# Row sums of the attention from one tile instead of two, and projections one step later

## The reference

```python
xn = layernorm(x)
c  = layernorm_64((xn @ W_to_kv.T) @ W_compress.T) * gamma + beta
q, k, v = rope(c @ Wq.T), rope(c @ Wk.T), c @ Wv.T
o  = softmax(causal(q @ k.T / 8)) @ v
z  = o @ W_comp2lat.T
out = x + z @ W_to_kv + z @ W_out.T + b_out + ffn(xn)   # ffn: shared part + 2 of 16 experts
```

## Time and profile before

| what | value |
|---|---|
| median of 3 runs | 1843.62 us (1842.06 to 1844.86) |
| the profiled execution | 1834.49 us |
| its span, first to last instruction | 1832.7 us |
| PE busy | 1759.1 us, 96% of the span |
| DVE busy | 1135.1 us, 62% |
| ACT busy | 752.7 us, 41% |
| POOL busy | 660.1 us, 36% |
| granted clock of TensorE, mean | 0.987 of full |

### The profile page before, as it was taken

One profiled execution on the slowest core, in us unless ns is written; L12 is line 12 of the kernel. 1 busy time (PEld: TensorE's weight loads), 2 busy tenths in 40 slices (PEclk: granted clock), 3 DMA queues, 4 the chain that ended last, 5 costly groups with the idle time before them and its releaser, 6 DMA issues. The chain is left out here.

```text
span 1832.7 us, 28109 instructions
## 1 busy us (share of the span) xinstructions
PE 1759.1 (96%) x8509; PEld 1406.6 (77%) x8509; DVE 1135.1 (62%) x2227; ACT 752.7 (41%) x1287; POOL 660.1 (36%) x676
## 2 busy tenths in 40 slices
PE   5699999999999998999999999999999989999998
PEld 4577877887777786778888877778888767777776
DVE  6776677777776753455555555555555436766676
ACT  3222222232222322333333343333333368888885
POOL 1544544444544442333434334333333321011110
PEclk9799999999999999999999999999999999999999
DMA  7757677766677756644545445555445438899896
GB/s 249 244 193 205 229 228 216 247 220 192 192 211 229 221 187 189 200 137 156 190 163 174 169 169 190 178 181 171 168 161 186 151 72 191 208 236 205 203 223 161
DMA packets 149581, 352.57 MB, mean 192 GB/s; under 512 B 19996, under 2 KB 41564, under 8 KB 149472
## 3 DMA queue, kind: packets, MB, share of 16 engines
q1 hardware_dynamic: 96924, 234.59, 38.9%
q0 software_dynamic: 43968, 104.91, 22.5%
q10 hardware_dynamic: 8580, 11.64, 2.3%
HBM read 208.30 MB, written 146.70 MB: 194 GB/s over the span
## 5 line engine op out<-in xcount | busy, mean ns | idle before, releaser
L1467 POOL DMA_INDIRECT expert_rows<-res,ids_all x143 | 149.8, 1048 | 444.7 <-ACT res L1289 435.8
L1408 DVE TENSOR_REDUCE mx<-emb 128x1 f32<-128x512 f32 (+3 forms) x288 | 175.1, 641 | 106.4 <-PE emb L1208 85.1
L69 PE MATMUL egu<-w,rT_0h 128*128 x576 | 186.4, 405 | 0.8 <-DVE rT_0l L1379 0.8
L69 PE MATMUL egu<-w,rT_1h 128*128 x568 | 182.6, 403 | 0.0
L1385 DVE TENSOR_TENSOR eh<-egu,esg 128x256 f32<-128x256 f32 x143 | 60.7, 425 | 183.5 <-ACT esg L1279 183.4
L1663 ACT ACTIVATE ex<-sc 128x1024 f32<-128x1024 f32 (+4 forms) x176 | 144.7, 822 | 55.0 <-PE sc L1608 47.3
L1015 POOL DMA_INDIRECT token_list<-tok,slot x128 | 128.5, 1004 | 104.9 <-DVE slot L730 69.0
L1462 POOL DMA_INDIRECT rows<-xn_scratch,rows_all x137 | 132.6, 968 | 48.1 <-issue 43.1
L1279 ACT ACTIVATE esg<-egu 128x256 f32<-128x256 f32 x143 | 54.9, 384 | 204.5 <-PE egu L69 201.7
L1728 POOL DMA_DIRECT2D base<-expert_rows x32 | 41.3, 1527 | 263.8 <-DMA base<-base_scratch 243.1
L1607 PE MATMUL sc<-qh,khl 128*128 128x512 f32 (+3 forms) x288 | 111.4, 387 | 9.2 <-ACT pr_2h L1663 2.4
(11 more groups left out here) (285 smaller groups left out, 4563.2 us busy)
## 6 DMA issues: line engine op xcount, KB each, us to landing
w<-expert_parts SPq DMA_DIRECT2D x64, 768.0 KB, 8.3
base<-expert_rows POOLq DMA_DIRECT2D x32, 1024.0 KB, 13.0
expert_parts<-ew_h SPq DMA_DIRECT2D x32, 768.0 KB, 5.9
expert_parts<-ew_l SPq DMA_DIRECT2D x32, 768.0 KB, 7.5
x<-x SPq DMA_DIRECT2D x16, 1024.0 KB, 6.3
xn_scratch<-xn SPq DMA_DIRECT2D x16, 1024.0 KB, 6.8
base_scratch<-xb SPq DMA_DIRECT2D x16, 1024.0 KB, 14.1
base<-base_scratch SPq DMA_DIRECT2D x16, 1024.0 KB, 6.3
```

Source lines behind the costliest of these rows:

```text
L69: mm = pe.matmul(dst, w, m, start=(first and i == 0), stop=(last and i == len(terms) - 1))
L1408: dve.tensor_reduce(mx[n % 2][:, j, c:c + 1], mb[g % 2][:, 0:width], AX.X, ALU.max).then_inc(m_red, 1)
L1467: pool.indirect_dma_start(parts_d[:, :], bass.IndirectOffsetOnAxis(ap=ids_all[:, t:t + 1], axis=0), res[t % 2][:, :], None, bounds_check=2 ...
```

## The change

The constant one moves from column 63 to column `ONE` = 32 of `vs`. The copy of the state into `vs` therefore has two pieces, columns 0 to 31 and 33 to 63. `fold` and `fold_inputs` follow: the copy of the folded weights is made before the column of beta is put in.

In `attend` the row sums lie in row 32 of `oT_h`. Behind `output_low` VectorE runs one more instruction of one row and 512 columns, which puts the low part of row 32 into row 96 of `oT_h`, a row of zeros until then; it waits for its predecessor over the new semaphore `o_low`, and it is now the one that raises `o_ev`. `last` has a one in row 32 and in row 96, made by two additions in place of one copy, and the matmuls with it run on `oT_h` alone: four in place of eight. `project_at` puts `project(k, 0)`, and with it the others and each `combine`, one iteration later.

```diff
-                dve.tensor_copy(vs[q][:, :, 0:C - 1], cn[:, :, 0, 0:C - 1]).then_inc(v_done, 1)
+                dve.tensor_copy(vs[q][:, :, 0:ONE], cn[:, :, 0, 0:ONE])
+                dve.tensor_copy(vs[q][:, :, ONE + 1:C], cn[:, :, 0, ONE + 1:C]).then_inc(v_done, 1)
...
-                free = max(free, final[k] + LAG + 2)
+                free = max(free, final[k] + LAG + 3)
...
                     for i in range(GT):
-                        for c in range(2):
-                            mm = pe.matmul(ob[k % 2][:, 2 * i:2 * i + 2], oT[k % 2][c][:, i * P:(i + 1) * P], last[:, :],
-                                           start=(c == 0), stop=(c == 1))
+                        mm = pe.matmul(ob[k % 2][:, 2 * i:2 * i + 2], oT[k % 2][0][:, i * P:(i + 1) * P], last[:, :], start=True, stop=True)
...
-                dve.tensor_tensor(oT[k % 2][1][:, :], ob[k % 2][:, :], value(oT[k % 2][0][:, :]), ALU.subtract).then_inc(o_ev, 1)
+                dve.tensor_tensor(oT[k % 2][1][:, :], ob[k % 2][:, :], value(oT[k % 2][0][:, :]), ALU.subtract).then_inc(o_low, 1)
+                dve.wait_ge(o_low, k + 1)
+                dve.tensor_tensor(oT[k % 2][0][C + ONE:C + ONE + 1, :], ob[k % 2][ONE:ONE + 1, :], value(oT[k % 2][0][ONE:ONE + 1, :]),
+                                  ALU.subtract).then_inc(o_ev, 1)
...
-            dve.tensor_copy(last[:, :], ident[:, C - 1:C + 1]).then_inc(ready, 1)
+            for i in range(2):
+                one = dve.tensor_tensor(last[:, i:i + 1], ident[:, ONE:ONE + 1], ident[:, C + ONE:C + ONE + 1], ALU.add)
+            one.then_inc(ready, 1)
```

More of the change, by code:

```diff
@@ L55 @@
 EH = EW // 2
-CA = C + 1
+ONE = C // 2
 def value(ap):
@@ L777, in first @@
                     dve.memset(powers[:, i, :], number)
-                dve.memset(vs[0][:, :, C - 1:C], 1.0)
-                dve.memset(vs[1][:, :, C - 1:C], 1.0).then_inc(setup, 1)
+                dve.memset(vs[0][:, :, ONE:ONE + 1], 1.0)
+                dve.memset(vs[1][:, :, ONE:ONE + 1], 1.0).then_inc(setup, 1)
                 norm_sums(0, 0)
@@ L1418, in fold_inputs @@
                 dve.wait_ge(fold_ev, 1)
-                dve.tensor_copy(fold[:, 0, C - 1:C], bet[:, :]).then_inc(fold_ev, 1)
+                dve.tensor_copy(fold[:, 1, :], fold[:, 0, :]).then_inc(fold_ev, 1)
                 dve.wait_ge(fold_ev, 2)
-                dve.tensor_copy(fold[:, 1, :], fold[:, 0, :]).then_inc(fold_ev, 1)
+                dve.tensor_copy(fold[:, 0, ONE:ONE + 1], bet[:, :]).then_inc(fold_ev, 1)
             def folded_low():
@@ L1515, in attend @@
         s_done, e_done, pv_done, low_done = sem("s_done"), sem("e_done"), sem("pv_done"), sem("low_done")
-        o_hi, o_ev = sem("o_hi"), sem("o_ev")
+        o_hi, o_low, o_ev = sem("o_hi"), sem("o_low"), sem("o_ev")
         l_done, l_ev, p_done, p_ev = sem("al_done"), sem("l_ev"), sem("p_done"), sem("p_ev")
@@ L1764, in shape_tables @@
     fold = np.eye(C, dtype=f)
-    fold[C - 1, :] = -1
-    fold[:, C - 1] = 0
+    fold[ONE, :] = -1
+    fold[:, ONE] = 0
     return np.eye(P, dtype=f), tri, np.concatenate([rev, start], axis=1), upto, token, tile_p, fold
```

## The result

The changed kernel takes 1834.86 us, median of 8 runs (1833.0 to 1839.18); the kernel before, beside it, 1844.14 us (1838.6 to 1847.46). The ratio is 0.9951, with an interval from 0.9936 to 0.9966: about 9 us faster. The forecast was 1848.6 us, slower, with a range from 1842.0 to 1853.5 us. It was wrong, in sign too.

A forecast was written before the change was run, and what follows sets the result against it. PE was taken to bound prepare and attend. 9.6 + 0.25 (prepare's last step and last's additions) - 6.8 + 1.6 + 0.3 = +4.95 us on the median 1843.62 gave 1848.6 us, range 1842.0 to 1853.5 us.

The forecast's parts named there:

- The bound of prepare: Prepare: PE, busy 600.6 of 625 us, sets the time, so nothing behind the second copy gives its cost back.
- The end of GpSimd's additions: Prepare: when GpSimd's four additions in a step end; the forecast had no term for a change in it.
- The turn-taking of the earlier trace: Prepare: VectorE and GpSimd alternate, one instruction each, so a second copy waits for one more addition, 1.28 us.
- The second turn: Prepare: the second copy's extra wait delays PE's third transpose in eleven of 13 steps, +9.6 us in all.
- The rival with a shared turn: Prepare: both copy halves share one turn, costing 0.5 us; the whole is -4.4 us, 1839.2 us; chance 0.15.
- The sums: Attend: 60 fewer matmuls with last in PE's flow, 0.113 us each, -6.8 us.
- The shift: Attend: projections one iteration later, some waits for o_ev shrink, others for exponentials and reciprocal arise, +1.6 us in sum.
- The tail: Behind the last outputs: the new row instruction adds 0.73 us, four sums fewer give back 0.45, +0.3 us.
- attend as a whole: Attend's sums, shift and tail together: forecast at 4.9 us shorter.

The follow-up runs named there:

- e5_before_sp: Kernel before, with the expert weights' store and load issued ahead of load_x(n + 2) on SyncE's queue in prepare: 1827.43 us, ratio 0.9935 to the kernel before.
- e1_before: The kernel before again, unchanged, for a second trace: 1846.15 us, ratio 0.9988 to the kernel before.
- e7: Changed kernel with one more GpSimd addition (128x176, into a tile nothing reads) ahead of the four in each prepare step: 1839.03 us, ratio 1.0002 to the kernel before.
- e4: The changed kernel again, unchanged, for a second trace: 1837.25 us, ratio 0.9939 to the kernel before.
- e3: Changed kernel with one copy of 63 columns into vs, ones in column 63, so its row sums are wrong: 1843.46 us, ratio 0.9973 to the kernel before.
- e2: Kernel before with only the copy into vs split in two pieces (32 and 31 columns): 1844.29 us, ratio 0.9977 to the kernel before.
- e10: Changed kernel with weights' store and load ahead of load_x on SyncE's queue, ones in column 0, one copy into vs: 1822.86 us, ratio 0.9927 to the kernel before.
- e8: Changed kernel with its projections back at the earlier iteration (LAG + 2 in place of LAG + 3): 1835.30 us, ratio 0.9982 to the kernel before.
- e11: e10 with its projections one iteration earlier (LAG + 2 in place of LAG + 3): 1824.25 us, ratio 0.9935 to the kernel before.
- e6: Changed kernel with the weights' store and load issued ahead of load_x(n + 2) on SyncE's queue: 1830.17 us, ratio 0.9950 to the kernel before.
- e9: e5_before_sp once more, beside other kernels on another chip: 1825.51 us, ratio 0.9945 to the kernel before.

## Why the prediction was wrong

**The bound of prepare: the step that failed.** The prediction said "both are bound by PE", and of the second copy "Nothing behind it gives this back: PE waits for nothing else in most of these steps". It read that from an execution in which TensorE waited little for anything else (7.4 us for `chs` and `h_l`; prepare loop 616.1 us) and took the 9 us between it and the median for something that "are no part of the change". What the runs showed in its place: SyncE's queue sets part of the steps. e5_before_sp shows it, by another order on the queue without touching an instruction: 606.6 us, 9.5 us below even the quick execution and 23.8 us below e1_before. So the steps had time in them that the second copy's wait could use up. The trace on which the prediction rests had the signs: SyncE's queue waits 208.4 us for the additions in it, and ScalarE 35.5 us for the weights, as in e1_before:
```profile
SPq L82 <- POOL xb L977: 208.4, 13, 18.2
```
That the loop closes through the end of GpSimd's additions rests on e7's sign and on ScalarE's waits; the share of the transfers themselves is open.

**The end of GpSimd's additions: the term left out.** The turn-taking of the earlier trace rows was applied to VectorE's instructions only, and the change of GpSimd's end stands in the sum at nothing, without a reason. The same turns move GpSimd: the additions end 0.5 us earlier in 13 steps. What this gave, less the second copy's wait, is known in bounds alone: 6.2 us by e4 against e3, with 4 runs of one, and 1.9 us by e2 against e1, where the whole is within their spread. e7 shows the sign from the other side.

**The second turn: right, and covered.** 1.32 us where 1.28 was forecast; counted from the start of the first copy the sum ends 1.18 us later; TensorE waits at the third transpose. +9.6 us was the forecast, 7.3 us is what the prepare loops of two kernels with the other order differ by (606.6 and 613.9 us), 8.6 us by e10. In the kernel as it is, this wait takes the place of others: those for `chs` and `h_l` are 17.2 us in e1_before and 6.2 us after, though only 7.4 us in the quick execution. The rival with a shared turn is refuted: that the kernel is faster came out, by another mechanism.

**The sums: right.** A group of eight matmuls and the step to the projection behind them took 0.81 us in most groups, the group of four 0.36 us: 0.445 us a group, 15 groups, 6.7 us for the 6.8 forecast. So the 0.113 us between two starts holds over the whole of attend, and not the 0.025 us that the prediction named beside it from the Trainium skill (TensorE: Matmul & The Clock Gate, section "Back-to-back issue gap"). That figure is the section's gap of a matmul by itself; for a stream with a weight load before each, the same section says that it is too low at small sizes.

**The shift: right in kind.** The row operation takes 686 ns (0.68 forecast):
```profile
L1695 DVE TENSOR_TENSOR oT_0h<-ob,oT_0h 1x512 fp32r<-1x512 f32 x8 | 5.5, 686 | 0.3
```
TensorE's waits in attend, after:
```profile
PE sc L1608 <- ACT pr_1h L1662: 5.4, 10, 1.1
PE sc L1608 <- ACT pr_3h L1662: 2.3, 6, 0.5
PE ob L1634 <- DVE oT_1h L1695: 2.1, 1, 2.1
PE sc L1608 <- DVE last L1711: 2.0, 1, 2.0
PE sc L1608 <- ACT pr_2h L1662: 1.8, 6, 0.3
PE sc L1608 <- ACT pr_0h L1662: 1.1, 1, 1.1
PE ob L1625 <- DVE lr L1702: 0.8, 2, 0.4
```
The waits for `o_ev` in the flow are gone (2.9 us in e1_before), those for ScalarE have grown: 1.11 us at k = 6, where 1.26 was forecast, and 0.40 us for the reciprocal of k = 0 and of k = 8, where 0.5 was forecast:
```profile
1540.27 0.47 PE L1625 MATMUL ob<-pr_2h,vhl 128*128 128x512 f32 x1 [0.40 <-DVE lr L1702]
...
1647.97 0.50 PE L1608 MATMUL sc<-qh,khl 128*128 128x512 f32 x1 [1.11 <-ACT pr_1h L1662]
```
All waits from the first to the last scores went from 12.0 us (e1_before) to 13.3 us: +1.3 for the forecast +1.6. Had the projections stayed an iteration earlier, the four waits for the low part ahead of the tail would be 5.8 us in place of 2.9 (e8, e11).

**The tail: mis-sized.** From the last scores to the end it is 11.6 us in e1_before and 14.1 us in the changed kernel, +2.5 us for the forecast +0.3. The wait is 0.7 us longer, as forecast; a projection (three matmuls) stands there in addition, for which the prediction had no term, and the clock is the rest (below). With the same attend it is 12.8 us in e6 and e7, where the clock was low for a shorter time. So attend as a whole, forecast at 4.9 us shorter, is 1.4 us shorter by the traces without a lower clock ahead of the tail (336.4 and 335.0 us), and 2.65 us is all that the medians of e10 and e9 differ by. Between the first and the last scores it is 324.7 us before and 321.0 us after. 6.7 us of sums and 0.7 us of the projection that moved to the tail, less 1.3 us of waits, leave 6.1 us, and 3.7 us are there: 2.4 us I cannot place. By their starts, the matmuls of scores and outputs took 3.3 us more in all, in steps too short to be shown as waits.

## What to carry to other kernels

Before a step is called bound by an engine, compare the profiled execution with the timed ones: where it is quicker than all of them, it may hide what binds the others, and a second profile of the same kernel helps. Read the waits of the other engines and of the queue too: here they were as long in the quick execution as in the slow one. Where a queue carries loads for several consumers, look for an issue that waits for something which those behind it don't need; here the order of three issues was worth 11 us, where the whole change gave 5.7 to 9.3 us. And where two engines take turns, cost an added instruction on both sides: it delays its own engine, and may free the other.

## What the runs showed of the hardware

GpSimd and VectorE alternate in both directions: a small extra addition of 128x176 took 696 ns in the mean in e7, where a third of 1349 ns would be 0.46 us, and a copy of 128x124 on VectorE took 1.32 us where its shortest took 0.22 us.

TensorE's granted clock fell in the tail. After its wait of 2.12 us the changed kernel's four sums start 0.21 us apart in place of 0.11, and its last eleven matmuls 0.43 us apart, where the earlier ones start 0.23 us apart; in e1_before, after a wait of 1.40 us, they do so from the third to the ninth, and the last three start 0.23 us apart again. The busy time of the last stretch of attend, in the changed kernel and in e1_before (length, then the engines, the clock third from the end), shows a mean clock of 0.58 and 0.70, between the two levels of 1.2 and 2.4 GHz:
```profile
1824.70:1832.80 8.10, 6.38 (x16) 4.45 (x16) 3.69 (x6) 0.00 (x0) 0.00 (x0) 0.58 0.58 225
```
```profile
1839.20:1844.90 5.70, 4.51 (x13) 2.96 (x12) 3.15 (x5) 0.00 (x0) 0.00 (x0) 0.70 0.50 194
```
The changed kernel shows this in all three of its traces. In e10_sp_one0, after the same wait of 2.12 us, the clock fell only behind the fourth of the twelve, and the tail took 12.8 us in place of 14.1. It is not the code: in e6_after_sp and e7_after_pool, whose attend is the changed kernel's, the sums start 0.11 us apart, the last two or three matmuls are quick again, and the tail took 12.8 us too. What decides it stays open.
